# Cross attention and an int4 feed-forward on one core: the turned half of k split into fp16 halves, the product M in fp16 alone, and two steps of TensorE's order moved

## What is computed

```python
def attn(q, k, v):                           # q = layernorm(x), k = v = ctx; [b, 128, 1024]
    qh = einsum('bcn,oc->bon', q, Wq).reshape(b, 8, 64, -1)
    kh = einsum('bcn,oc->bon', k, Wk).reshape(b, 8, 64, -1)
    vh = einsum('bcn,oc->bon', v, Wv).reshape(b, 8, 64, -1)
    qh = softmax(qh, axis=-2) * 64 ** -0.5
    kh = softmax(kh, axis=-1)
    context = einsum('bhdn,bhen->bhde', kh, vh)
    out = einsum('bhde,bhdn->bhen', context, qh).reshape(b, 512, -1)
    out = einsum('bcn,oc->bon', out, Wo) + bo[None, :, None]
    norm = maximum(sqrt(sum(out * out, axis=1, keepdims=True)), 1e-12)
    return out / norm * g * sqrt(128)
x = x + attn(layernorm(x), ctx, ctx)
w = (nibbles(qweight) - round(zeros / scales).T) * scales.T        # [1024, 1024]
x = x + layernorm(x) @ w + bias
```

## Time and profile before

| | |
|---|---|
| median of 3 runs | 634.06 us (633.74 to 636.24) |
| the profiled execution | 635.1 us, of which the span from first to last instruction is 633.3 us |
| mean granted clock of TensorE | 0.987 of full speed |
| PE, matmuls | 596.1 us busy, 94% of the span, 3431 instructions |
| POOL | 548.9 us, 87% |
| DVE | 543.2 us, 86% |
| ACT | 507.1 us, 80% |
| DMA | 96.19 MB, 152 GB/s |

### The profile page before, as it was taken

How to read it: one execution, slowest core, us unless ns; L and a number is a source line. 1 busy time by engine, 2 the same in 40 slices (tenths; PEclk the granted TensorE clock), 3 DMA queues, 4 the chain that set the end, 5 groups by cost and what they waited for, 6 DMA issues and landing times.

```text
span 633.3 us, 10844 instructions
## 1 busy us (share of the span) xinstructions
PE 596.1 (94%) x3431; PEld 380.6 (60%) x3447; DVE 543.2 (86%) x904; ACT 507.1 (80%) x789; POOL 548.9 (87%) x473
## 2 busy tenths in 40 slices
PE   4686799999999999999999999999999999998897
PEld 3454375656657575665657566665756666574654
DVE  4897789898988999888988988898898989889754
ACT  4888789797879879787988979797897978788442
POOL 4268879999999999999999999999899999999630
PEclk9888799999999999999999999999999999999999
DMA  9416658868596876868887885868698595848551
GB/s 324 108 36 147 120 140 152 208 97 208 116 151 184 157 189 129 187 125 171 167 138 184 142 202 117 179 143 141 182 152 198 121 194 116 154 116 162 111 141 67
DMA packets 246969, 96.19 MB, mean 152 GB/s; under 512 B 236136, under 2 KB 237952, under 8 KB 246912
## 3 DMA queue, kind: packets, MB, share of 16 engines
q1 hardware_dynamic: 240576, 72.42, 59.3%
q10 hardware_dynamic: 6336, 23.07, 10.7%
HBM read 28.85 MB, written 8.39 MB: 59 GB/s over the span
## 4 chain that ended last, share of the span: by engine, by line
PE 74%; DVE 9%; ACT 5%; issue 4%; DMA 3%; POOL 3%; SPq 1%; ACTq 0%; POOLq 0%; DVEq 0%
PE ps_m L1619 14%; PE ps_m L1493 7%; PE ps_k L1411 4%; PE ps_o L1503 4%; PE ps_o L1411 4%; PE ps_o L1412 4%; PE ps_o L1413 4%; PE ps_k L1413 4%; PE ps_k L1412 4%; PE ps_q L1411 3%; PE ps_q L1413 3%; PE ps_q L1412 3%; PE ps_ta L1472 2%; PE ps_o L1527 2%; PE ps_tb L1472 2%
## 5 line engine op out<-in xcount | busy, mean ns | idle before, releaser
L514 POOL TENSOR_TENSOR q_tok_lo<-q_exp,q_tok_hi 128x1024 f16<-128x1024 f32 x64 | 135.8, 2132 | 8.1 <-ACT q_tok_hi L748 7.3
L737 ACT ACTIVATE q_exp<-q_exp,w_unit 128x512 f32<-128x512 f32 x128 | 92.9, 726 | 53.4 <-DVE q_exp L1070 53.3
L486 POOL TENSOR_TENSOR q_exp<-q_exp,q_rec 128x1024 f32<-128x1024 f32 x63 | 119.9, 1904 | 4.9
L1065 DVE TENSOR_REDUCE q_nmax<-ps_q 128x8 f32<-128x512 f32 x128 | 86.9, 679 | 28.5 <-PE ps_q L1413 28.2
L1619 PE MATMUL ps_m<-w_int,x_parts 128*128 128x512 f16 x432 | 100.0, 379 | 0.3 <-DMA x_parts<-spare 0.2
L1070 DVE TENSOR_TENSOR q_exp<-ps_q,q_nmax 128x512 f32<-128x512 f32 x128 | 88.5, 692 | 4.4
L522 POOL TENSOR_TENSOR k_lo<-k_exp,k_hi 128x1024 f16<-128x1024 f32 x32 | 82.2, 2569 | 9.2 <-ACT k_hi L678 9.2
L1056 DVE TENSOR_REDUCE k_nmax<-ps_k 128x1 f32<-128x1024 f32 x64 | 77.1, 1205 | 5.2 <-PE ps_k L1413 4.9
L1493 PE MATMUL ps_m<-k_t,c_t 128*128 128x256 f32 x256 | 77.0, 383 | 0.0
L1077 DVE TENSOR_REDUCE q_sum<-q_exp 128x16 f32<-128x1024 f32 x64 | 76.9, 1201 | 0.0
L748 ACT ACTIVATE q_tok_hi<-q_exp 128x1024 f16<-128x1024 f32 x64 | 67.5, 1054 | 7.8 <-POOL q_exp L486 5.4
(11 more groups left out here) (221 smaller groups left out, 1461.7 us busy)
## 6 DMA issues: line engine op xcount, KB each, us to landing
x_res<-in_x ACTq DMA_DIRECT2D x16, 512.0 KB, 3.6
out_x<-y SPq DMA_DIRECT2D x15, 512.0 KB, 2.9
x_in<-in_x ACTq DMA_DIRECT2D x14, 512.0 KB, 4.8
c_in<-in_ctx ACTq DMA_DIRECT2D x14, 512.0 KB, 6.0
x_in<-in_x SPq DMA_DIRECT2D x2, 512.0 KB, 5.6
c_in<-in_ctx SPq DMA_DIRECT2D x2, 512.0 KB, 7.0
q_hi<-q_tok_hi SPq DMA_TRANSPOSE x64, 3.3
q_lo<-q_tok_lo SPq DMA_TRANSPOSE x64, 3.3
```

Source lines behind the costliest of these rows:

```text
L486: nc.gpsimd.tensor_tensor(pair, pair, rec.unsqueeze(2).to_broadcast([P, 2 * HEADS, DH]), ALU.mult).then_inc(qs_done, 1)
L514: nc.gpsimd.tensor_tensor(q_tok_lo[p % 2][:], q_exp[:, 2 * p:2 * p + 2, :].rearrange("p t d -> p (t d)"), q_tok_hi[p % 2][:], ALU.subtract ...
L737: nc.scalar.activation(q_exp[:, j, :], q_exp[:, j, :], ACT.Exp, scale=w_unit[:]).then_inc(qexp_done, 1)
L1065: nc.vector.tensor_reduce(q_nmax[:, j, :], heads, op=ALU.max, axis=AX_X, negate=True).then_inc(qmax_done, 1)
```

## The change

Chunks 2 and 3 of k get what chunks 0 and 1 have. Their exponentials are lifted too (`PARTED = 4` takes the place of `TURNED = 2` where the bias is made). ACT's `move_tk` writes the turned chunk as fp16 into `k_t_hi`, and a new step of DVE, `low_tk`, subtracts that from PSUM and writes `k_t_lo`. The fp32 copies `k_t` and `c_t` go, and with them one of `move_tc`'s two activations per half. `mix_m` becomes three fp16 matmuls of 512 columns per block. PE's transposes, which reuse `ps_ta` and `ps_tb`, wait for `low_tk` as well as for `move_tk`, and so does `mix_m`.

Two orders change. On PE `project_q(4)` and `project_q(5)` follow one another behind the last pass of half 0, and the two transposes of chunk 3 stand between the two passes of half 1. On DVE `low_tk(0)`, `low_tk(1)` come after `scale_y(0)`, and `shift_q(5)`, `low_tk(2)`, `low_tk(3)` ahead of `scale_y(1)`. Iteration 0 is changed likewise. The core of the diff:

```diff
 def exp_k(b, sums, j):                         # ACT
-    if j < TURNED:
+    if j < PARTED:
...
 def move_tk(k):                                # ACT
-    nc.scalar.activation(k_t[:, t0:t0 + 4, fc * P:(fc + 1) * P],
+    fc = fc + TURNED
+    nc.scalar.activation(k_t_hi[:, t0:t0 + 4, fc * P:(fc + 1) * P],
...
 def move_tc(h):                                # ACT
     nc.scalar.activation(c_t_hi[1 - s][:, 4 * h:4 * h + 4, :], turned, ACT.Identity,
-                         scale=c_fit[:]).then_inc(cthi_done, 1)
-    nc.scalar.activation(c_t[1 - s][:, 4 * h:4 * h + 4, :], turned, ACT.Identity,
                          scale=c_fit[:]).then_inc(tc_moved, 1)
...
+def low_tk(k):                                 # DVE
+    t0, fc = 4 * (k % 2), TURNED + k // 2
+    dve.wait_ge(tk_moved, TK * a + k + 1)
+    if k == 0 and begun(a):
+        dve.wait_ge(m_ready, a)
+    part = (slice(None), slice(t0, t0 + 4), slice(fc * P, (fc + 1) * P))
+    nc.vector.tensor_tensor(k_t_lo[part], (ps_ta, ps_tb)[k % 2][:].rearrange("p (t c) -> p t c", t=4),
+                            k_t_hi[part], ALU.subtract).then_inc(tklo_done, 1)
...
                     pick_nibbles(2)            # DVE, iteration 0
-                    pick_nibbles(3)
+                    low_tk(0)
+                    low_tk(1)
                     shift_q(3)
                     set_up_gains()
                     shift_q(4)
+                    low_tk(2)
+                    low_tk(3)
                     set_up_top()
+                    pick_nibbles(3)
...
                     scale_y(0)                 # DVE, the other iterations
+                low_tk(0)
+                low_tk(1)
                 if do_n:
                     abs_c()
                 shift_q(4)
                 invert_k()
                 sum_q(a, 1)
+                shift_q(5)
+                low_tk(2)
+                low_tk(3)
                 if do_f and i != END:
                     scale_y(1)
-                shift_q(5)
...
 def transpose_k(k):                            # PE; transpose_c, mix_m and spread_last_rs likewise
         pe.wait_ge(tk_moved, TK * a + k - 1)
+        pe.wait_ge(tklo_done, TS * a + k - 1)
...
 def mix_m(t0, t1):                             # PE
-        three(ps_m[:, 0:TURNED * P], c_t_hi[s][:, t, :], c_t_lo[s][:, t, :], k_t_hi[:, t, :],
-              k_t_lo[:, t, :], start=(t == 0), stop=False)
-        last = nc.tensor.matmul(ps_m[:, TURNED * P:], c_t[s][:, t, :], k_t[:, t, :], start=False,
-                                stop=(t == TC - 1))
+        last = three(ps_m[:], c_t_hi[s][:, t, :], c_t_lo[s][:, t, :], k_t_hi[:, t, :], k_t_lo[:, t, :],
+                     start=(t == 0), stop=(t == TC - 1))
...
                     project_q(3)               # PE, iteration 0
+                    project_q(4)
                     transpose_k(2)
                     transpose_k(3)
-                    project_q(4)
+                    project_q(5)
                     set_up_spread()
-                    project_q(5)
                     mix_m(0, 4)
...
                     feed_forward(0, (1,))      # PE, the other iterations
+                project_q(4)
+                project_q(5)
+                if do_f and i != END:
+                    feed_forward(1, (0,))
                 transpose_k(2)
-                project_q(4)
                 transpose_k(3)
                 if do_f and i != END:
-                    feed_forward(1, (0, 1))
-                project_q(5)
+                    feed_forward(1, (1,))
                 if do_c:
                     mix_out(1)
```

More of the change, by code:

```diff
@@ L50 @@
 TURNED = 2
+PARTED = 4
 PAIRS = STEPS // 2
@@ L110, in build @@
         c_lo = sb("c_lo", [P, N], F32R)
-        c_t = [sb(f"c_t{s}", [P, TC, P]) for s in range(2)]
         c_t_hi = [sb(f"c_t_hi{s}", [P, TC, P], F16) for s in range(2)]
@@ L140, in build @@
         k_lift = sb("k_lift", [P, 1])
-        k_bias = sb("k_bias", [P, TURNED])
+        k_bias = sb("k_bias", [P, PARTED])
         k_hi = [sb(f"k_hi{j}", [P, N], F16) for j in range(TURNED)]
         k_lo = [sb(f"k_lo{j}", [P, N], F16) for j in range(TURNED)]
-        k_t_hi = sb("k_t_hi", [P, TC, TURNED * P], F16)
-        k_t_lo = sb("k_t_lo", [P, TC, TURNED * P], F16)
-        k_t = sb("k_t", [P, TC, HID - TURNED * P])
+        k_t_hi = sb("k_t_hi", [P, TC, PARTED * P], F16)
+        k_t_lo = sb("k_t_lo", [P, TC, PARTED * P], F16)
         q_tok_hi = [sb(f"q_tok_hi{r}", [P, 2 * HID], F16) for r in range(2)]
@@ L252, in build @@
         tk_moved = sem("tk_moved")
+        tklo_done = sem("tklo_done")
         tc_ready = sem("tc_ready")
@@ L263, in build @@
         cfit_steps = sem("cfit_steps")
-        cthi_done = sem("cthi_done")
         ctlo_done = sem("ctlo_done")
@@ L320, in build @@
         TK = 2 * (HC - TURNED)
+        TS = 2 * (PARTED - TURNED)
         def pipeline(iteration):
@@ L661, in exp_k @@
                                              bias=k_lift[:]).then_inc(kbias_done, 1)
-                        act.wait_ge(kbias_done, TURNED * b + j + 1)
+                        act.wait_ge(kbias_done, PARTED * b + j + 1)
                         bias = k_bias[:, j:j + 1]
@@ L1053, in max_k @@
                         dve.wait_ge(kexp_done, 4 * (b - 1) + j + 1)
-                    if begun(b) and j < TURNED:
-                        dve.wait_ge(kbias_done, TURNED * (b - 1) + j + 1)
+                    if begun(b) and j < PARTED:
+                        dve.wait_ge(kbias_done, PARTED * (b - 1) + j + 1)
                     nc.vector.tensor_reduce(k_nmax[:, j:j + 1], ps_k[:], op=ALU.max, axis=AX_X,
@@ L1446, in transpose_c @@
                         pe.wait_ge(tk_moved, TK * n + h - 1)
+                        pe.wait_ge(tklo_done, TS * n + h - 1)
                     for t in range(4):
@@ L1481, in mix_m @@
                         pe.wait_ge(tk_moved, TK * (a + 1))
+                        pe.wait_ge(tklo_done, TS * (a + 1))
                         pe.wait_ge(tc_moved, 2 * (a + 1))
@@ L1591, in spread_last_rs @@
                     pe.wait_ge(tk_moved, TK * NB)
+                    pe.wait_ge(tklo_done, TS * NB)
                     nc.tensor.matmul(ps_ta[:, 0:P], rs_parts[:].rearrange("p g r -> p (g r)"), ident16[:],
```

## The result

The changed kernel takes 721.4 us (median of 4 runs, 719.5 to 724.1), the kernel before 635.1 beside it. The ratio is 1.136, with a 95% interval of 1.130 to 1.141. The forecast was 704 with a range of 672 to 724, and 0.95 for slower.

A forecast was written before the change was run, and what follows sets the result against it. PE was taken to bound the kernel. Per full iteration -0.94 + 3.96 + 0.2 + 2.0 = +5.22, times 13 = +67.9, plus 2 elsewhere, on 635.1 gives 705.0; forecast 704 us, range 672 to 724.

The forecast's parts named there:

- The gap, 3.96 per iteration: Mid-iteration, PE waits at project_q(5) for DVE's shift_q(4): a chain of 4.61 us beside only 0.65 of PE work.
- The clock, 2.0: Behind the gap PE loses its clock; the slower dense work costs 2.0 us per iteration, bounds nothing and 3.0.
- the clock stays up: Rival: PE keeps its clock behind the gap, +44 us, 678 us in all; chance 0.15.
- M, -0.94: Eight blocks of M per iteration as three fp16 matmuls of 512 columns, 0.65 each instead of 0.765, save 0.94 us.
- a microsecond taken from PE counts in full: PE bounds the steady iterations, so a microsecond added to or taken from its queue counts in full, 13 times.
- charging nothing for these two: low_tk(2) and low_tk(3) on DVE fall into PE's mix_out(1), 2.6 us long, at no cost; 1.2 without that cover.
- The bias of the third chunk, +0.2: The added k_bias before the third chunk's exponential on ACT delays project_k(3) by 0.2 us, bounds 0 to 0.33.
- Iterations 0 and 1: +0.5 and +1.2: Iteration 0: low parts ahead of shift_q(3), later set_up_top, about +0.5 us. Iteration 1: later project_q(5), transposes following, about +1.2.
- The heavier clock: Rival: the clock stays down longer in every iteration or falls again: 717 us, 725 to 735; beyond 724 chance 0.06.
- M does not get shorter: Rival: M's three 512-column matmuls with new weights run slower than the projection's, adding 12 us, 716 us; chance 0.02.

The follow-up runs named there:

- experiment 1: Changed kernel with project_q(5) put back behind the second pass of half 1 on PE; 652.9 us, ratio 1.024.
- experiment 2: Kernel before with only the changed order of PE's middle in iterations 1 to 15, no low parts, old M; 693.1 us, ratio 1.088.
- experiment 4: Changed kernel with shift_q(4) ahead of low_tk(0), low_tk(1) and abs_c on DVE; 664.3 us, ratio 1.048.
- experiment 3: Changed kernel with 16 extra matmuls, result thrown away, between project_q(4) and project_q(5) in the full iterations; 694.9 us, ratio 1.092.
- experiment 5: Kernel before with M in fp16 alone, low parts of chunks 2 and 3 left out, orders of before; 632.6 us, ratio 0.996.
- experiment 12: Experiment 5 with DVE's low_x2 made an instruction with one input instead of two; 633.8 us, ratio 0.996.
- experiment 6: Experiment 5 with the move of M (m_t) ahead of the next entry's second-chunk exponential on ACT; 635.6 us, ratio 1.004.
- experiment 9: Experiment 5 with the third sum of q moved behind the next entry's second maximum on DVE; 655.4 us, ratio 1.030.
- experiment 7: Experiment 1 with the move of M (m_t) ahead of the next entry's second-chunk exponential on ACT; 651.4 us, ratio 1.027.
- experiment 10: Experiment 7 with the third sum of q moved behind the next entry's second maximum on DVE; 664.6 us, ratio 1.044.
- experiment 11: Kernel before with only the third sum of q moved behind the next entry's second maximum on DVE; 655.9 us, ratio 1.031.
- experiment 8: Whole change with better orders on PE, DVE and ACT, and shift_q(3) ahead of the low parts in iteration 0; 647.5 us, ratio 1.021.

## Why the prediction was right, and which terms were off

**The gap, 3.96 per iteration: right.** The timeline shows 3.78 to 3.85 of idle time in all 13, counted from the end of the last record, which reaches 0.16 beyond the point where the next matmul could have started. From start to start, as I counted, it is 3.94: 416.83 less 412.24, the start of `project_q(4)`, less 0.65. The two low parts advance DVE by 0.59 and 0.60 (0.61 taken), `abs_c` by 1.12 and `shift_q(4)` by 1.41. Experiments 1, 2 and 4 show that the order makes the gap, on either engine.

**The clock, 2.0: right as a mean.** 2.0 by experiment 3, and a stretch at the lower clock stands behind the gap in every full iteration. But it is 1.6 in nine iterations and 2.8 in four, where the lower clock lasts longer; the prediction's 2.0 was itself the mean of stretches of both kinds (1.6 to 3.0). That the two mixtures agree so closely is luck. Why every third iteration pays more is open. That the clock stays up is excluded for the changed kernel; the range's lower part was for that case.

**M, -0.94: the mechanism was right, the size wrong.** The blocks are 0.65 apart, and PE's busy time falls from 36.12 to 35.26 (experiments 5 and 12). But of 0.94 only 0.3 comes out of the iteration (experiment 5, 36.00 instead of 36.30 in most). The step that failed is the sentence that a microsecond taken from PE counts in full. The place can be read: all eight blocks of M lie between PE's sum of squares for the norm and `mix_g`. That stretch is 13.72 us long before (334.85 to 348.57) and 13.41 after (428.50 to 441.91), 13.41 in experiment 5 and 13.40 in experiment 12. From the norm on DVE (`n`) to the second maximum it is 8.07 before and 8.07 to 8.08 in those three, with no gap in DVE's queue; in the three without the old M ACT's exponential, `m_t` and the start of `mix_g` follow 3.40 after that maximum has begun. So a second chain of nearly the same length ran beside PE's. PE, DVE and ACT before, in rows that the prediction does not use:

```profile
334.85 1.89 PE L1503 MATMUL ps_o<-ones,sq 128*128 128x1 f32 x16
...
348.57 1.09 PE L1527 MATMUL ps_o<-vo,m_t 128*64 128x128 f32 x16
```

```profile
336.78 0.17 DVE L1119 TENSOR_SCALAR n<-ps_o 128x8 f32<-128x8 f32 x1 [0.51 <-PE ps_o L1503]
...
344.85 1.21 DVE L1056 TENSOR_REDUCE k_nmax<-ps_k 128x1 f32<-128x1024 f32 x1
```

```profile
347.83 0.69 ACT L781 ACTIVATE m_t<-ps_m,g_fit 128x512 f32<-128x512 f32 x1 [0.20 <-PE ps_m L1493]
```

ACT came to `m_t` 0.2 us before M was ready. That was about the whole margin: the stretch gets 0.31 shorter (13.72 to 13.41), and the rest of 0.94 turns into a wait. Against the forecast 0.63 of 0.94 is lost, 13 times: 8.2 us. Experiments 6 and 9 confirm the place: with `m_t` ahead of the exponential the stretch is 12.80, nearly all of 0.94 shorter, and with 1.45 us less in DVE's queue it is 12.88. Both times the gain is lost again elsewhere in the iteration.

**DVE's low parts cost more than their place in the gap.** With the gap gone (experiment 1) DVE reaches `n` 2.61 us after the start of PE's sum of squares instead of 1.93, since its queue has had no pause since `shift_q(5)`. That makes the wait before `mix_g` 1.30 instead of 0.72, 0.6 of the 1.0 by which an iteration of experiment 1 is longer than one of experiment 5 (37.03 and 36.00). Another 0.30 is not DVE's low parts but PE's order: the first pass of half 1 now stands right behind `project_q(4)` and has to wait for `scale_y(0)`. The rest is the bias, next. In the changed kernel itself it doesn't show: there DVE is idle for 3.48 before `low_tk(2)` and reaches `n` after 1.93, so that charging nothing for these two was right as long as the gap is there.

**The bias of the third chunk, +0.2,** measured 0.13. The waits do not show it, but the distance from `mix_g` to the first transpose of k does, with `project_k(2)` and `project_k(3)` between: 7.17 to 7.19 in kernels without the bias (before and experiments 2, 5 and 12), 7.29 to 7.33 in those with it (the changed kernel and experiments 1, 3 and 4).

**Per iteration** 5.69 came instead of 5.22, 74.0 instead of 67.9 for the 13. Against the 36.30 of most iterations, from which the prediction counted, it is 5.79; with the sizes above, -0.31 + 3.94 + 0.13 + 2.0, the sum is 5.76.

**Iterations 0 and 1: +0.5 and +1.2 forecast, +7.9 and +2.5 measured.** The first `mix_g` stands at 58.15 instead of 50.22. PE in iteration 0:

```profile
38.53 0.61 PE L1428 MATMUL ps_q<-wq_hi,xn_lo 128*128 128x512 f16 x1 [4.00 <-DVE q_exp L1069]
...
58.15 1.09 PE L1545 MATMUL ps_o<-vo,m_t 128*64 128x128 f32 x16 [2.03 <-ACT m_t L780]
```

I priced the two low parts at their duration and didn't follow PE's order there: `project_q(4)` was put ahead of the transposes of chunk 3, so the low parts ahead of `shift_q(3)` have nothing beside them. In experiment 2, which has iteration 0 as before and no low parts, the first `mix_g` is at 49.59; with the change's iteration 0 (experiments 4 and 7) at 55.32 and 55.17. So the low parts and PE's order there cost 5.6 together; no run separates them. The other 3 us in the changed kernel come from before that. Kernels with the same iteration 0 differ by up to 5 us: 58.2 to 60.4 in the changed kernel and experiments 1, 3 and 10, where one small instruction of DVE takes eight to ten times its length, and 55.2 and 55.3 in experiments 7 and 4, where none does. The last section tells how.

**The rivals.** The clock that stays up would have given 678: excluded by the windows. The heavier clock was priced at 717. It came in four of the 13 iterations, and the mean of the clock is as forecast; the 18 us by which the profiled execution lies over 705.0 are in the terms above (6.1 in the 13 iterations, 8.7 in iterations 0 and 1) and behind iteration 14 (3.2). "M does not get shorter" (716) came near the effect for a wrong reason: the matmuls are as fast as the projection's, and two thirds of what they leave free is waited away.

**The range** held in part by luck. The room above 704 was made for a longer stretch at the lower clock; what filled it are M's saving and iterations 0 and 1, for which the prediction left little.

**What stays open.** M's saving is held back first by DVE's queue between the norm and the second maximum, with ACT's exponential at its end. With that shortened something else takes the gain: in experiment 9 the holding of `low_x2`, which grew, in experiment 6 ACT's exponentials at `project_k(2)` and `project_k(3)`. Taking out the holding alone left the first (experiment 12). Whether taking out several together frees the saving was not tried.

## What to carry to other kernels

A wait that is hidden belongs to the work that hides it: before a step is moved, count what the chain needs from its trigger to its use (here 4.6 us) and what the new order leaves beside it (0.65). In a kernel in which several engines stand at 80 to 94%, an engine's full busy share does not say that its microsecond counts; look at the next place where it meets another engine and read from that one's timeline how early the other arrived. What a change saves beyond that margin comes back as a wait at that place.

## What the runs showed of the hardware that was not expected

DVE's instruction with two inputs in SBUF and POOL's operations hold each other off, and the one that comes second waits for the other's end. `low_x2` takes 1.24 us before in most iterations, 1.58 in experiment 5, 2.02 in 6, 2.39 in 7 and 2.86 in 11, only because it starts at another moment of POOL's operation, and POOL's operation behind it takes 1.0 us longer each time. With one input both effects are gone (1.21 and 2.14, experiment 12). The Trainium skill, page "SBUF — State Buffer", section "Who interferes with whom", says that a DVE instruction with two SBUF inputs contends with a GpSimd instruction that reads SBUF, and that the lock on the shared ports is exclusive; the traces agree. The same section counts DVE's `tensor_scalar` among the instructions that can take the ports shared with GpSimd. In the start of the changed kernel, a small one of 8x128 elements:

```profile
19.61 0.21 DVE L1009 TENSOR_SCALAR m_t<-m_t 8x128 f32<-8x128 f32 x1
19.86 2.08 DVE L1011 TENSOR_SCALAR m_t<-m_t 8x128 f32<-8x128 f32 x1
```

```profile
19.74 2.13 POOL L522 TENSOR_TENSOR k_lo<-k_exp,k_hi 128x1024 f16<-128x1024 f32 x1 [5.89 <-ACT k_hi L678]
```

It begins 0.12 us after POOL's `k_lo` and ends where that ends, ten times as long as its neighbour of the same shape; in the kernel before it took 0.22, ahead of POOL. The maximum behind it waits as long, and PE's `project_k` at 25.03 stands still for 3.33 us; in experiment 4, where the instruction took 0.22, that wait is 1.04. In experiments 1, 3 and 8 another one of 8x128, a `tensor_tensor` with two inputs in SBUF, comes just behind the start of `k_lo` and takes 2.23 instead of 0.28.
